# The last residual addition of a fused block, moved from GpSimd into an adding DMA

## The chip, the cores and the metric

The kernel runs on one core of one Trainium2 chip. The metric is the device time of one launch in microseconds (us), lower is better. A profile of one execution on the chip stands beside the times; lines such as L2083 are lines of the kernel before.

## What is computed

The input x has 8192 tokens of 512 numbers in float32. Two halves follow one another, each with a norm before it, a norm behind it and the residual:

```python
x = x + layernorm(attn(layernorm(x)))   # after this line x is called x1 here
x = x + layernorm(ffn(layernorm(x)))    # this is the output
```

`attn` is a gated state mixer: an input projection to u and v, silu of v, a depthwise convolution over three tokens, a linear recurrence along the tokens, a gate u * silu(y), an output projection with a bias, the residual of its own input and a layer norm with weight and bias. `ffn` is 512 to 2048 to 512 with weights made ternary (-1, 0, 1) on the chip, biases and an exact gelu between. The last line is where the change lies: output = x1 + norm of the FFN's result.

## The kernel before, in words

The tokens are cut into NT = 16 tiles of 512, each tile into NB = 4 blocks of 128 tokens (the partitions). A program of stages s runs over the tiles; in stage s four tiles are in work at once, given by `tiles(s)`: tile fa = s-2 is in the FFN, tile c = s-1 in the attention half, tile n = s+1 is loaded, normed and projected, and tile e = s-3 is finished. Each engine has its own list of instructions in a fixed order; times such as AT_F_NORM only set the order in which the list is written. Engines wait for each other by semaphores alone, with constants.

TensorE does all matmuls: `f1` (512 to 2048, reads the transposed operand x3T), `f2` (2048 to 512, into four PSUM banks f2b), and for the attention half `u`, `v` and `o`. Activations are split into a high and a low float16 part, so each product is done twice (three times in the attention half). VectorE makes the low parts (`lo`, L807), statistics, the taps and scan of the recurrence, the norms, and x1 (L963). ScalarE does gelu, high parts, silu, and the affine forms of norms. GpSimd does small scales (L2037, L2038), the carried states (L2088), the output projection's bias (`add_bias`, L2093) and the last addition (`finish`, L2083). SyncE issues all DMAs.

Two buffers matter. `xs` has X_SLOTS = 4 slots, one per tile in flight: x is loaded there, VectorE writes x1 over it (semaphore x1_ok), then makes the norm of x1 in `hb` (n3_ok), which is split, transposed by DMA into x3T and read by f1 of the next stage. `hb` has four blocks and is used in turns: first by tile c (residual copy by ScalarE, L1661, bias, output of `o`, norms), later by tile e: VectorE writes the FFN's result from PSUM (`f_add`, L820), ScalarE norms it in place (`ffn_norm`, L1631, semaphore fn_ok), GpSimd adds x1 from xs in place (`finish`, semaphore fin_ok), SyncE stores it (`store`, L398, semaphore out_st), and only after that store may ScalarE write the residual copy of the next tile c into the block (L1660 waits for out_st).

SyncE's order in a stage is: four stores of tile e, each waiting for its addition; the load of tile n = e+4 into the slot of tile e (`load_x`, L362, waits for all four additions); four transposes of the first operand of tile n; four transposes of x3 of tile c (L414). The last tile is different: its last addition is done by VectorE (`last_sum`, `last_out`, semaphore fin_last) and its stores come at the end.

Of the kernel before, what the change touches and what calls it, by code (L numbers as in the profile page):

```python
# [27 lines left out]
NB = TT // P  # L28
# [63 lines left out]
def build(nc, x, w_in, w_out, w1t, w2t, params, rows, out):  # L92
# [23 lines left out]
    with ExitStack() as ctx:  # L116
# [3 lines left out]
        def sem(name):  # L120
# [99 lines left out]
        w1_in = [sem(f"w1_in{q}") for q in range(4)]  # L220
        w2_in = [sem(f"w2_in{i}") for i in range(4)]
        w1_back, w2_back = sem("w1_back"), sem("w2_back")
        out_st = [sem(f"out_st{i}") for i in range(NB)]

        const_ok, prep, pmx, pm1, scale_ok = sem("const_ok"), sem("prep"), sem("pmx"), sem("pm1"), sem("scale_ok")
# [24 lines left out]
            sem("x1_ok"), sem("n3_ok"), sem("x3_hi"), sem("x3_lo"))  # L250

        f2_sum, fin_last, xc_ok, cen_ok = sem("f2_sum"), sem("fin_last"), sem("xc_ok"), sem("cen_ok")
        f1_mm, gelu_ok, hh_ok, hl_ok, f2_mm, f_ok, fn_ok, fin_ok = (
            sem("f1_mm"), sem("gelu_ok"), sem("hh_ok"), sem("hl_ok"), sem("f2_mm"), sem("f_ok"),
            sem("fn_ok"), sem("fin_ok"))

        def tiles(s):

# [99 lines left out]
        @block.sync  # L358
        def _(sp):
            def load_x(t):  # L360
                if t >= X_SLOTS:
                    sp.wait_ge(fin_ok, NB * (t - X_SLOTS + 1))  # L362
                if t == X_SLOTS - 1:
                    sp.wait_ge(w_ok, last_of(W1_CHUNK, range(8, 12)))
                sp.dma_start(xs[:, t % X_SLOTS, :, :], x_d[t]).then_inc(x_in[t % X_SLOTS], 16)

            def load_w1(q):

                sp.dma_start(w1_raw[q], w1_d[q]).then_inc(w1_in[q], 16)

            def load_w2(group):

                if group == 0:
                    sp.wait_ge(abs_ok, 4)
                elif group == 1:
                    sp.wait_ge(x1_lo, 3 * NB)
                elif group == 2:
                    sp.wait_ge(win_l, 2 * KC)
                else:
                    sp.wait_ge(wo_l, KC)  # L380
                sp.dma_start(w2_raw[group], w2_d[group]).then_inc(w2_in[group], 16)

            def reload_w1():

                sp.wait_ge(w_ok, last_of(W2_CHUNK, range(4, 8)))
                sp.dma_start(w1_kept[3], w1_d[3]).then_inc(w1_back, 16)

            def reload_w2():

                sp.wait_ge(w_ok, last_of(W2_CHUNK, range(8, 12)))  # L390
                sp.dma_start(w2_kept[3], w2_d[3]).then_inc(w2_back, 16)

            def store(t, j):
                if t < NT - 1:
                    sp.wait_ge(fin_ok, NB * t + j + 1)
                else:
                    sp.wait_ge(fin_last, j + 1)
                sp.dma_start(out_d[t, j], hb[:, j, :]).then_inc(out_st[j], 16)  # L398

            def transpose(kind, t, j):  # L400

                if kind == "t1":
                    dst, split = x1T[:, t % 2], x1_lo
                    if t > 1 and j == 0:
                        sp.wait_ge(u_mm, KC * (t - 1))
                else:
                    dst, split = x3T_of(t), x3_lo
                    if t == NT - 2 and j == 0:
                        sp.wait_ge(u_mm, KC * (t + 1))
                    elif t > 0 and j == 0:  # L410
                        sp.wait_ge(f1_mm, FC * min(t, NT - 2))
                r = block_no[kind, t, j] % T_SLOTS
                sp.wait_ge(split, NB * t + j + 1)
                sp.dma_start_transpose(dst[:, :, j * P:(j + 1) * P],  # L414
                                       tp[:, r].rearrange("p h d -> p (h d)")).then_inc(transposed[r], 16)

            def transposes(kind, t):
                for j in range(NB):
                    transpose(kind, t, j)

            sp.dma_start(par[:, :], params).then_inc(par_in, 16)
            for j in range(NB):
                sp.dma_start(xs[:, 0, j, :], x_d[0, :, j, :]).then_inc(x0_in[j], 16)
            for k in range(KC):
                sp.dma_start(wf[:, k, D:], w_in_d[:, k, D:]).then_inc(win_in[k], 16)
            for i in range(2):
                sp.dma_start(xs[:, 1, 2 * i:2 * i + 2, :], x_d[1, :, 2 * i:2 * i + 2, :]).then_inc(x1_in[i], 16)
            transposes("t1", 0)
            for i in range(2):
                sp.dma_start(wf[:, 2 * i:2 * i + 2, 0:D], w_in_d[:, 2 * i:2 * i + 2, 0:D]).then_inc(winu_in[i], 16)  # L430
            transposes("t1", 1)
            load_x(2)
            sp.dma_start(wo_raw, w_out_d).then_inc(wout_in, 16)
            load_w1(0)
            load_w1(1)
            sp.dma_start(row[:, :, :], rows.partition_broadcast(P)).then_inc(row_in, 16)
            load_w1(2)
            load_w1(3)
            load_w2(2)
            transposes("t1", 2)  # L440
            load_w2(0)
            load_w2(1)
            load_w2(3)
            load_x(3)
            reload_w1()
            transpose("t1", 3, 0)
            transpose("t1", 3, 1)
            transpose("t1", 3, 2)
            transpose("t1", 3, 3)
            reload_w2()  # L450
            transpose("t3", 1, 0)
            transpose("t3", 1, 1)
            transpose("t3", 1, 2)
            transpose("t3", 1, 3)
            for s in range(3, NT + 2):
                _, c, n, e = tiles(s)
                if e is not None:
                    for j in range(NB):
                        store(e, j)
                    if e + X_SLOTS < NT:  # L460
                        load_x(e + X_SLOTS)
                if n is not None:
                    transposes("t1", n)
                if c is not None:
                    transposes("t3", c)
            for j in range(NB):
                store(NT - 1, j)
            for j in range(NB):
                sp.wait_ge(out_st[j], 16 * NT)


        @block.tensor
# [1129 lines left out]
        def _(act):  # L1602
# [50 lines left out]
            def residual(c, j):  # L1653

                if c == NT - 1:
                    act.wait_ge(fin_ok, NB * (NT - X_SLOTS + 1))
                else:
                    act.wait_ge(x3_lo, NB * (c - 1) + j + 1)
                if 1 < c < NT - 1:
                    act.wait_ge(out_st[j], 16 * (c - 1))  # L1660
                act.activation(hb_of(c)[:, j, :], xs[:, c % X_SLOTS, j, :], ACT.Identity, bias=nm1[:, c % 4, j:j + 1],  # L1661
                               scale=rs1[:, c % 4, j:j + 1]).then_inc(res_ok, 1)
# [362 lines left out]
        def _(pool):  # L2025
# [54 lines left out]

            def finish(e, j):
                pool.wait_ge(fn_ok, NB * e + j + 1)
                pool.tensor_tensor(hb[:, j, :], hb[:, j, :], xs[:, e % X_SLOTS, j, :], ALU.add).then_inc(fin_ok, 1)  # L2083

            def keep_state(c, b):
                i = KC * c + b
# [183 lines left out]
```

## Time and profile before

| | us |
|---|---|
| median of 3 runs | 1421.73 |
| lowest and highest run | 1421.04, 1422.21 |
| span of the profiled execution, first to last instruction | 1420.3 |
| own time of the profiled execution beside its span | not given by the page |
| TensorE busy | 1400.8 |
| VectorE busy | 1116.8 |
| ScalarE busy | 878.2 |
| GpSimd busy | 422.3 |
| mean granted TensorE clock | 0.999 |
| DMA traffic | 82.00 MB |

The times are those of the whole launch; the profile is of one execution. Busy time is the union of an engine's instruction intervals. Matmuls overlap in the pipeline: one is shown with 0.38 us, while the next starts 0.22 us later. DMA issues are listed as the queue of the engine that issues them (SPq for SyncE), with the time from issue to landing.

### The profile page before, as it was taken

To read this page: it belongs to the slowest core of one execution; us is meant where nothing else is said; L and a number is where in the kernel's file an instruction comes from. 1 tells how busy PE (TensorE), PEld (TensorE's weight loads), DVE (VectorE), ACT (ScalarE), POOL (GpSimd) and SP (SyncE) were. 2 spreads that over 40 slices of the span, in tenths; PEclk is the share of its full clock that TensorE was granted. 3 is DMA by queue.
4 is the path that set the end of the run, shared out by engine and by line. 5 is a ranking of instruction groups with operands and counts; after the bars stand their busy time and mean duration, and the time that the engine had idled before them with its cause. 6 is when DMAs were issued, how large, how long until landed. Compare 5 with 4: busy or idle time off the path is not lost.

```text
span 1420.3 us, 18989 instructions
## 1 busy us (share of the span) xinstructions
PE 1400.8 (99%) x6506; PEld 640.0 (45%) x6506; DVE 1116.8 (79%) x1889; ACT 878.2 (62%) x1264; POOL 422.3 (30%) x522
## 2 busy tenths in 40 slices
PE   7999999999999999999999999999999999999997
PEld 4444444444444444444444444444444444444443
DVE  7999987868779686796867878677796877998744
ACT  7999665656556565675656756565565656753443
POOL 5234241322314232042331413223142321523221
PEclk9999999999999999999999999999999999999999
DMA  8703221211311122121311203113111221001200
GB/s 245 254 36 90 60 83 20 78 30 38 82 30 60 30 61 59 30 66 25 89 30 31 82 16 82 31 38 82 31 60 30 53 67 30 30 1 30 60 31 30
DMA packets 155984, 82.00 MB, mean 58 GB/s; under 512 B 132720, under 2 KB 132720, under 8 KB 155760
## 3 DMA queue, kind: packets, MB, share of 16 engines
q1 hardware_dynamic: 155888, 80.79, 22.0%
q8 instruction: 51, 0.84, 0.2%
q14 instruction: 45, 0.37, 0.1%
HBM read 31.49 MB, written 16.78 MB: 34 GB/s over the span
## 4 chain that ended last, share of the span: by engine, by line
PE 85%; DVE 4%; issue 3%; POOL 1%; ACT 0%; POOLq 0%; DVEq 0%; ACTq 0%
PE f2b L581 14%; PE f2b L582 14%; PE f1b L552 14%; PE f1b L553 14%; PE misc L520 6%; PE misc L519 6%; PE misc L518 6%; PE misc L533 3%; PE misc L534 3%; PE misc L532 3%; DVE bn L789 1%; DVE vl L865 0%; DVE vl L874 0%; DVE ring L807 0%; POOL rsc L2038 0%
## 5 line engine op out<-in xcount | busy, mean ns | idle before, releaser
L581 PE MATMUL f2b<-w,ring 128*128 128x512 fp8e5 x1004 | 380.5, 379 | 1.2 <-DVE ring L807 0.9
L582 PE MATMUL f2b<-w,ring 128*128 128x512 fp8e5 x1004 | 380.5, 379 | 0.0
L552 PE MATMUL f1b<-x3T,w 128*128 128x512 f16 x960 | 363.8, 379 | 0.1
L553 PE MATMUL f1b<-x3T,w 128*128 128x512 f16 x960 | 363.8, 379 | 0.0
L1610 ACT ACTIVATE ring<-f1b,par 128x512 f32<-128x512 f32 x256 | 175.2, 684 | 227.8 <-PE f1b L553 227.5
L2037 POOL TENSOR_SCALAR ve<-mv 128x4 f32<-128x4 f32 (+2 forms) x89 | 35.4, 398 | 725.5 <-DVE mv L799 725.4
L807 DVE SCALAR_TENSOR_TENSOR ring<-ring,f_sc 128x512 f16<-128x512 f32 x256 | 212.5, 844 | 37.6 <-ACT ring L1620 37.4
L1620 ACT ACTIVATE ring<-ring,f_sc 128x512 f16<-128x512 f32 x256 | 180.1, 710 | 0.0
L518 PE MATMUL misc<-x1T,win_hi 128*128 128x512 f16 x456 | 172.8, 379 | 0.0
L520 PE MATMUL misc<-x1T,win_lo 128*128 128x512 f16 x456 | 172.8, 379 | 0.0
L519 PE MATMUL misc<-x1T,win_hi 128*128 128x512 f16 x456 | 172.8, 379 | 0.0
L581 PEld LDWEIGHTS f2b<-w,ring 128*128 128x128 f16 x1004 | 98.2, 98 | 121.1 <-DVE ring L807 2.4
L582 PEld LDWEIGHTS f2b<-w,ring 128*128 128x128 f16 x1004 | 98.2, 98 | 118.0
L552 PEld LDWEIGHTS f1b<-x3T,w 128*128 128x128 fp8e5 x960 | 93.9, 98 | 114.4 <-issue 1.5
L553 PEld LDWEIGHTS f1b<-x3T,w 128*128 128x128 fp8e5 x960 | 93.9, 98 | 112.7
L1729 ACT ACTIVATE vb<-misc,par,inv_sig 128x512 f32<-128x512 f32 x54 | 41.9, 776 | 140.3 <-PE misc L520 140.1
L789 DVE BATCH_NORM_STATS2 bn<-hb 128x6 f32<-128x512 f32 x184 | 118.8, 679 | 0.2
L865 DVE SCALAR_TENSOR_TENSOR vl<-vb,par,vl 128x512 f32<-128x512 f32 x128 | 105.9, 866 | 0.9 <-POOL vb L2142 0.8
L2093 POOL TENSOR_TENSOR hb<-hb,row 128x512 f32<-128x512 f32 x56 | 80.7, 1444 | 85.7 <-ACT hb L1661 85.7
L2083 POOL TENSOR_TENSOR hb<-hb,xs 128x512 f32<-128x512 f32 x60 | 99.6, 1687 | 18.6 <-ACT hb L1631 18.6
L532 PE MATMUL misc<-wo_hi,g_hi 128*128 128x512 f16 x240 | 91.0, 379 | 0.4 <-DVE g_lo L909 0.3
L533 PE MATMUL misc<-wo_lo,g_hi 128*128 128x512 f16 x240 | 91.0, 379 | 0.0
(227 smaller groups left out, 2015.3 us busy)
## 6 DMA issues: line engine op xcount, KB each, us to landing
out_dram<-hb SPq DMA_DIRECT2D x64, 256.0 KB, 2.0
xs<-x_dram SPq DMA_DIRECT2D x14, 1024.0 KB, 5.4
ring<-w1t_dram SPq DMA_DIRECT2D x3, 1024.0 KB, 13.2
stage<-w2t_dram SPq DMA_DIRECT2D x3, 1024.0 KB, 8.0
x1T<-tp SPq DMA_TRANSPOSE x68, 3.1
xs<-x_dram SPq DMA_DIRECT2D x4, 256.0 KB, 3.4
stage<-w_in_dram SPq DMA_DIRECT2D x4, 256.0 KB, 5.7
xs<-x_dram SPq DMA_DIRECT2D x2, 512.0 KB, 7.2
```

The lines of the kernel that those rows point to most:

```text
L518: pe.matmul(o[:, :], wh, x1T[:, s_, k, :], start=k == 0, stop=False)
L519: pe.matmul(o[:, :], wh, x1T[:, s_, KC + k, :], start=False, stop=False)
L520: mm = pe.matmul(o[:, :], wl, x1T[:, s_, k, :], start=False, stop=k == KC - 1)
L532: pe.matmul(out_[:, :], g_hi[:, k, js], wo_hi[:, k, :], start=c > 0 and k == 0, stop=False)
L533: pe.matmul(out_[:, :], g_hi[:, k, js], wo_lo[:, k, :], start=False, stop=False)
L552: pe.matmul(b[:, :], w, src[:, k, :], start=k == 0, stop=False)
L553: mm = pe.matmul(b[:, :], w, src[:, KC + k, :], start=False, stop=k == KC - 1)
L581: pe.matmul(f2b[q][:, :], h_hi[:, i % H_SLOTS, qs], w2[:, j, :], start=j == 0, stop=False)
L582: mm = pe.matmul(f2b[q][:, :], h_lo[:, i % H_SLOTS, qs], w2[:, j, :], start=False, stop=j == FC - 1)
L807: ve_.scalar_tensor_tensor(out=h_lo[:, i % H_SLOTS, :], in0=gg[:, i % G_SLOTS, :], scalar=f_sc[:, 0:1], in1=h_hi[:, i % H_SLOTS, :], op0=A ...
L1610: act.activation(gg[:, i % G_SLOTS, :], f1b[i % 2][:, :], ACT.Gelu, bias=par[:, B1 + j:B1 + j + 1], scale=1.0 / ACT_SCALE).then_inc(gelu_o ...
L1620: act.activation(h_hi[:, i % H_SLOTS, :], gg[:, i % G_SLOTS, :], ACT.Copy, scale=f_sc[:, 0:1]).then_inc(hh_ok, 1)
```

## The change

Before, tile e's result was normed in `hb`, x1 was added to it there by GpSimd, and the sum was stored. Now SyncE stores x1 itself to the output as soon as VectorE has made it (`store_x1`), in the stage in which tile c = s-1 is in the attention half. Two stages later GpSimd issues, for each block, a DMA that adds the normed FFN result from `hb` onto what stands in the output (`accum_op=ALU.add`); before issuing it waits for fn_ok as before and for the landing of that block's x1 store. The landing of the adding DMA now counts out_st. The last tile keeps its old way, with a semaphore of its own (last_st). Since GpSimd no longer reads `xs`, the load of tile t into a slot waits only for the norm (n3_ok) and the x1 store (x1_st) of the tile before in that slot; the same holds for the residual copy of the last tile, which uses a slot of xs.

```diff
--- before.py
+++ after.py
@@ -220,6 +220,8 @@
         w1_in = [sem(f"w1_in{q}") for q in range(4)]
         w2_in = [sem(f"w2_in{i}") for i in range(4)]
         w1_back, w2_back = sem("w1_back"), sem("w2_back")
+        x1_st = [sem(f"x1_st{i}") for i in range(NB)]
+        last_st = [sem(f"last_st{i}") for i in range(NB)]
         out_st = [sem(f"out_st{i}") for i in range(NB)]
 
         const_ok, prep, pmx, pm1, scale_ok = sem("const_ok"), sem("prep"), sem("pmx"), sem("pm1"), sem("scale_ok")
@@ -250,9 +252,9 @@
             sem("x1_ok"), sem("n3_ok"), sem("x3_hi"), sem("x3_lo"))
 
         f2_sum, fin_last, xc_ok, cen_ok = sem("f2_sum"), sem("fin_last"), sem("xc_ok"), sem("cen_ok")
-        f1_mm, gelu_ok, hh_ok, hl_ok, f2_mm, f_ok, fn_ok, fin_ok = (
+        f1_mm, gelu_ok, hh_ok, hl_ok, f2_mm, f_ok, fn_ok = (
             sem("f1_mm"), sem("gelu_ok"), sem("hh_ok"), sem("hl_ok"), sem("f2_mm"), sem("f_ok"),
-            sem("fn_ok"), sem("fin_ok"))
+            sem("fn_ok"))
 
         def tiles(s):
 
@@ -359,7 +361,9 @@
         def _(sp):
             def load_x(t):
                 if t >= X_SLOTS:
-                    sp.wait_ge(fin_ok, NB * (t - X_SLOTS + 1))
+                    sp.wait_ge(n3_ok, NB * (t - X_SLOTS + 1))
+                    for j in range(NB):
+                        sp.wait_ge(x1_st[j], 16 * (t - X_SLOTS + 1))
                 if t == X_SLOTS - 1:
                     sp.wait_ge(w_ok, last_of(W1_CHUNK, range(8, 12)))
                 sp.dma_start(xs[:, t % X_SLOTS, :, :], x_d[t]).then_inc(x_in[t % X_SLOTS], 16)
@@ -390,12 +394,16 @@
                 sp.wait_ge(w_ok, last_of(W2_CHUNK, range(8, 12)))
                 sp.dma_start(w2_kept[3], w2_d[3]).then_inc(w2_back, 16)
 
-            def store(t, j):
-                if t < NT - 1:
-                    sp.wait_ge(fin_ok, NB * t + j + 1)
-                else:
-                    sp.wait_ge(fin_last, j + 1)
-                sp.dma_start(out_d[t, j], hb[:, j, :]).then_inc(out_st[j], 16)
+            def store_x1(t):
+
+                for j in range(NB):
+                    sp.wait_ge(x1_ok, NB * t + j + 1)
+                    sp.dma_start(out_d[t, j], xs[:, t % X_SLOTS, j, :]).then_inc(x1_st[j], 16)
+
+            def store_last(j):
+
+                sp.wait_ge(fin_last, j + 1)
+                sp.dma_start(out_d[NT - 1, j], hb[:, j, :]).then_inc(last_st[j], 16)
 
             def transpose(kind, t, j):
 
@@ -442,31 +450,34 @@
             load_w2(1)
             load_w2(3)
             load_x(3)
+            store_x1(0)
             reload_w1()
             transpose("t1", 3, 0)
             transpose("t1", 3, 1)
             transpose("t1", 3, 2)
             transpose("t1", 3, 3)
             reload_w2()
+            store_x1(1)
             transpose("t3", 1, 0)
             transpose("t3", 1, 1)
             transpose("t3", 1, 2)
             transpose("t3", 1, 3)
             for s in range(3, NT + 2):
                 _, c, n, e = tiles(s)
-                if e is not None:
-                    for j in range(NB):
-                        store(e, j)
-                    if e + X_SLOTS < NT:
-                        load_x(e + X_SLOTS)
+                if e is not None and e + X_SLOTS < NT:
+                    load_x(e + X_SLOTS)
                 if n is not None:
                     transposes("t1", n)
+                if c is not None and c < NT - 1:
+                    store_x1(c)
                 if c is not None:
                     transposes("t3", c)
             for j in range(NB):
-                store(NT - 1, j)
+                store_last(j)
             for j in range(NB):
-                sp.wait_ge(out_st[j], 16 * NT)
+                sp.wait_ge(x1_st[j], 16 * (NT - 1))
+                sp.wait_ge(out_st[j], 16 * (NT - 1))
+                sp.wait_ge(last_st[j], 16)
 
 
         @block.tensor
@@ -1653,7 +1664,8 @@
             def residual(c, j):
 
                 if c == NT - 1:
-                    act.wait_ge(fin_ok, NB * (NT - X_SLOTS + 1))
+                    act.wait_ge(n3_ok, NB * (NT - X_SLOTS + 1))
+                    act.wait_ge(x1_st[j], 16 * (NT - X_SLOTS + 1))
                 else:
                     act.wait_ge(x3_lo, NB * (c - 1) + j + 1)
                 if 1 < c < NT - 1:
@@ -2080,7 +2092,8 @@
 
             def finish(e, j):
                 pool.wait_ge(fn_ok, NB * e + j + 1)
-                pool.tensor_tensor(hb[:, j, :], hb[:, j, :], xs[:, e % X_SLOTS, j, :], ALU.add).then_inc(fin_ok, 1)
+                pool.wait_ge(x1_st[j], 16 * (e + 1))
+                pool.dma_start(out_d[e, j], hb[:, j, :], accum_op=ALU.add).then_inc(out_st[j], 16)
 
             def keep_state(c, b):
                 i = KC * c + b
```

## Rows read from the trace of the kernel before

**Rows 1.** The page's busy line: us, share of the span, instructions
```profile
PE 1400.8 (99%) x6506; PEld 640.0 (45%) x6506; DVE 1116.8 (79%) x1889; ACT 878.2 (62%) x1264; POOL 422.3 (30%) x522
```

**Rows 2.** Busy us by stretch, as the first line says
```profile
...
core 0: us, PE busy (x) PEld busy (x) DVE busy (x) ACT busy (x) POOL busy (x), PEclk, DMA share, GB/s
425.70:512.00 86.30, 86.30 (x401) 39.14 (x400) 67.09 (x112) 52.60 (x76) 24.72 (x30) 1.00 0.20 49
170.00:1400.00 1230.00, 1228.55 (x5688) 555.71 (x5687) 949.10 (x1569) 731.92 (x1064) 354.34 (x414) 1.00 0.19 46
1400.00:1420.30 20.30, 12.87 (x60) 5.66 (x58) 11.69 (x20) 4.74 (x7) 5.56 (x14) 0.92 0.14 52
```

**Rows 3.** Groups by line: busy us, mean ns, idle us before
```profile
...
L2083 POOL TENSOR_TENSOR hb<-hb,xs 128x512 f32<-128x512 f32 x60 | 99.6, 1687 | 18.6 <-ACT hb L1631 18.6
...
L2093 POOL TENSOR_TENSOR hb<-hb,row 128x512 f32<-128x512 f32 x56 | 80.7, 1444 | 85.7 <-ACT hb L1661 85.7
```

**Rows 4.** GpSimd in order of time: start, us, [idle before <- releaser]
```profile
...
437.60 6.76 POOL L2083 TENSOR_TENSOR hb<-hb,xs 128x512 f32<-128x512 f32 x4 [0.93 <-ACT hb L1631]
...
458.91 0.56 POOL L2037 TENSOR_SCALAR ve<-mv 128x4 f32<-128x4 f32 x1 [8.29 <-DVE mv L799]
```

**Rows 5.** SyncE's queue in order of time, 425.7 to 512
```profile
...
438.90 5.82 SPq L398 DMA_DIRECT2D out_dram<-hb  x4
444.76 0.43 SPq L365 DMA_DIRECT2D xs<-x_dram  x1
...
504.20 5.53 SPq L414 DMA_TRANSPOSE x3T<-tp  x4
```

**Rows 6.** VectorE's line L807: ns min/median/max
```profile
...
L807 DVE SCALAR_TENSOR_TENSOR ring<-ring,f_sc x256: 710/739/1756, 97.5 to 1404.5; 128x512 f16<-128x512 f32 x128
```

**Rows 7.** Transpose at 1026.5, its landing, TensorE behind it
```profile
...
L414 SPq DMA_TRANSPOSE x3T<-tp x1: 1822/1822/1822, 1026.5 to 1026.5; - x1
...
DMA to landing us min/median/max: 3.7/3.7/3.7
...
1029.98 0.38 PE L582 MATMUL f2b<-w,ring 128*128 128x512 fp8e5 x1
1030.45 0.38 PE L552 MATMUL f1b<-x3T,w 128*128 128x512 f16 x1
```

**Rows 8.** DMA issues: KB each, median us to landing
```profile
...
out_dram<-hb SPq DMA_DIRECT2D x64, 256.0 KB, 2.0
xs<-x_dram SPq DMA_DIRECT2D x14, 1024.0 KB, 5.4
```

**Rows 9.** ScalarE in order of time, one stage
```profile
...
436.71 1.52 ACT L1631 ACTIVATE hb<-hb,nm,rs 128x512 f32<-128x512 f32 x2 [0.17 <-POOL nm L2069]
...
463.40 0.80 ACT L1661 ACTIVATE hb<-xs,nm,rs 128x512 f32<-128x512 f32 x1
...
470.10 0.80 ACT L1661 ACTIVATE hb<-xs,nm,rs 128x512 f32<-128x512 f32 x1
```

**Rows 10.** VectorE in order of time, the same stage
```profile
...
477.72 0.75 DVE L928 SCALAR_TENSOR_TENSOR hb<-misc,o_inv,hb 128x512 f32<-128x512 f32 x1 [1.16 <-PE misc L534]
...
495.20 0.74 DVE L963 SCALAR_TENSOR_TENSOR xs<-hb,rsc,xs 128x512 f32<-128x512 f32 x1
```

**Rows 11.** Transpose at 508.4, its landing, TensorE's next f1
```profile
...
L414 SPq DMA_TRANSPOSE x3T<-tp x1: 1340/1340/1340, 508.4 to 508.4; - x1
...
DMA to landing us min/median/max: 3.2/3.2/3.2
...
512.05 0.38 PE L552 MATMUL f1b<-x3T,w 128*128 128x512 f16 x1
```

**Rows 12.** SyncE's queue at the front, the transpose's landing
```profile
...
25.98 1.24 SPq L414 DMA_TRANSPOSE x1T<-tp  x1
27.27 0.58 SPq L365 DMA_DIRECT2D xs<-x_dram  x1
...
DMA to landing us min/median/max: 3.1/3.1/3.1
```

## The prediction, made before the change was run

> **What bounds the kernel now.** I read the profile from the whole down to single instructions. The busy line of the page comes first: TensorE is busy 1400.8 us (99%) of a span of 1420.3, the next engine (VectorE) 79% [rows 1]. The busy times by stretch come second, because an average hides where the idle 19.5 us lie: one whole stage, 425.7 to 512.0, is 86.30 us of TensorE in 86.30; the long middle from 170 to 1400 leaves it idle for 1230.00 - 1228.55 = 1.45 us; the end from 1400 leaves 20.30 - 12.87 = 7.43; the remaining 10.6 lie before 170, in the loading and weight preparation [rows 2]. So the reader sees a kernel in which every other engine works behind TensorE. GpSimd's 60 additions are 99.6 us in total [rows 3].
>
> **What goes.** In each of 15 tiles GpSimd loses 4 additions, 6.76 us together (437.60 to 444.36) [rows 4]. Who waited for them: SyncE's queue, which stored the four blocks and then loaded the next x [rows 5], and, through the stores' landing, ScalarE's residual copy into the same buffer. While they ran, some of VectorE's `lo` instructions were slow: the median is 0.739 us, the longest 1.756 [rows 6]. VectorE gets some microseconds a stage back. That is worth nothing inside a stage whose TensorE is full, and at most the 1.45 us of idle time in the middle all together. I take 0.1 us of gain.
>
> **What comes, on GpSimd.** 60 DMA issues, one for each addition. The trace has no DMA issued by GpSimd, so its time on that engine is bounded from rows of other engines: 0.43 us, SyncE's issue of the x load (its four stores fill 5.82 us only because they wait for the additions in between), and 1.82 us, the longest issue of a transpose [rows 5, 7]. I take 1.3 us, nearer the upper end, since GpSimd's own addition of the same block is 6.76 / 4 = 1.69. Four are 5.2 us in place of 6.76. GpSimd's next task that others wait for starts at 458.91 (the scale of the next x), so even 4 us each would be hidden [rows 4]: 437.60 + 16 = 453.6, and 5.3 us are left for the four one-column state copies that come between. Cost on the path 0. The added wait in front of each, that the x1 store has landed, is for a store of two stages (some 150 us) earlier, so it holds nobody up.
>
> **What comes, in the transfer.** The adding DMA must land before the residual copy of the same block number overwrites `hb`. Plain stores land 2.0 us after issue and 1 MB loads 5.4 [rows 8]; an adding DMA moves 256 KB but must also read its destination, so I take twice a store, 4 us, and keep 2.0 and 5.4 as bounds. The first block is normed from 437.5 on, and the residual copies of the first and the fourth start at 463.40 and 470.10 [rows 9]. With four at 1.3 + 4 us, even one after another, the last lands at 437.6 + 21.2 = 458.8. Cover for the last: 11 us; for the first more than 20. Cost 0.
>
> The Trainium skill (DMA: Bandwidth & Descriptors, Anatomy of one DMA) prices one GpSimd DMA at 2.0 us plus bytes over 436 GB/s; by that estimate a block takes 2.6 us, and the sum stays the same. The skill also has a rule against the change (SBUF: State Buffer, in the box on VectorE blocking DMA): while VectorE runs an instruction in a two-port mode, GpSimd can't write its descriptors, and its DMA waits to the end of that instruction. The two-port candidates here are the plain tensor_scalar instructions, which run near the end of the stage; in the window of the finish VectorE runs scalar_tensor_tensor [rows 6]. If each issue waited for one instruction of 1.756 us, four would be 7 us late, inside the 11 of cover. So rule and row differ only in the size of a hidden cost.
>
> **What moves on SyncE.** (a) Four x1 stores a tile are issued once x1 exists: the last is written by VectorE at 495.20 + 0.74 = 495.9, the first transpose of the next operand is issued at 504.20 [rows 5, 10]. With 0.43 us for an issue and 2.0 to land, they are done by 498.4. Cover 5.8 us; without it, each microsecond would be one microsecond of TensorE. (b) The four stores at 438.90 vanish from SyncE's queue, and with them the wait for the additions, behind which the x load stood. (c) The x load of the next tile loses its wait altogether: it is issued right behind the fourth transpose of x3, some 20 us earlier in the stage. That gains nothing: its old landing (444.76 + 5.4 = 450.2) was already ahead of GpSimd's scale for that tile at 458.91 [rows 4, 5]. The queue's count is the same plus the 60 adding DMAs, which go to a queue of GpSimd; 15.7 MB more are written and as many read back, against a DMA share of 0.19 in the middle [rows 2], so that even twice the traffic would leave more than half of the DMA engines' time idle.
>
> **The narrow place** is (c). The fourth transpose is issued at 508.4 and lands 3.2 us later, at 511.6; TensorE's first f1 matmul of the next tile starts at 512.05, without a gap [rows 11]. How much room is that? One stage answers: there the landing took 3.7 us from 1026.5, and the f1 matmul came 0.47 us after its predecessor instead of 0.22, a gap of 0.25 [rows 7]. So the room is 3.7 - 3.2 - 0.25 = 0.25 us. A 1 MB load placed directly behind the transpose could use it up. The nearest row speaks against it: at 25.98 a transpose was followed at 27.27 by a 1 MB x load, the very order of the change, and landed in 3.1 us [rows 12]. From below the cost is 0, since nothing lands earlier by it; from above, a landing as late as the load's own 5.4 would cost 12 x (5.4 - 3.2 - 0.25) = 23 us, for the loads of tiles 4 to 15. I take 0, going by the row with the same order.
>
> **The sum.** -0.1 (VectorE) + 0 (GpSimd issue) + 0 (landing) + 0 (stores and loads on SyncE) on a span of 1420.3 gives 1420.2. The profile gives no other time for its execution; the median of the runs shown is 1421.73, so 1.4 us are put down to what lies around the span. Together 1421.6, which is 0.1 under that median.
>
> **Rivals.**
> 1. *The x load delays the last x3 transpose (slower).* Place: the stage border, 12 times. It decides from 0.25 us of delay. At 0.5 us it costs 12 x 0.25 = 3.0, at 1.0 us 9.0: 1424.7 to 1430.7. For it: almost no room. Against it: [rows 12]. Chance 0.10.
> 2. *The adding DMA is slow and the residual copy waits (slower).* The fourth residual copy at 470.10 may slip until its own 0.80 us and its bias addition on GpSimd (1.44) still meet VectorE's use at 477.72 [rows 3, 9, 10]: to 475.5. So it decides from (475.5 - 437.6) / 4 = 9.5 us a block. At 12 us a block the fourth lands at 485.6, 10 us late in each of 13 stages: about 1550. For it: no such DMA in the trace. Against it: it would have to be nearly twice the landing of a transfer four times as large. Chance 0.07.
> 3. *A first DMA queue of GpSimd costs something once, at start or end.* Nothing in the trace prices it; by the nearest rows, one more landing of 3.2 to 5.4 us that nobody overlaps: 1424.8 to 1427.0. Chance 0.08.
> 4. *Faster.* All idle time of the middle gives 1.45 us, which isn't told from no change; over 2.8 us would have to come from the front or from the tail, whose last tile is unchanged. Chance 0.03, at about 1418.
> The forecast itself has 0.72.
>
> **From these to the numbers.** What a measurement of this kernel can tell from no change is about 0.2%, 2.8 us, so 1418.9 to 1424.6. Forecast: same, 0.72. Slower: rivals 1 to 3, 0.25. Faster: 0.03. The range runs from 1420.0 (all the idle time of the middle gone) to 1427.5, which takes in rival 3 and the smaller half of rival 1 and leaves out some 15 in 100.
>
> **What would show it.** In the changed profile: TensorE's busy time within 1 us of 1400.8, and its idle time in 170 to 1400 below 2 us. GpSimd's line for the additions is gone; VectorE's busy sum is lower by 20 to 50 us, its `lo` mean (844 ns before) nearer 740. The adding DMAs land within 5.4 us, and ScalarE's residual copies show no wait for a DMA. SyncE issues the x load next to the last x3 transpose, whose landing stays at 3.2 to 3.3. I am wrong if a wait of TensorE for those transposes appears in more than one stage (rival 1), if ScalarE waits at the residual copy (rival 2), or if the time around the span grows beyond 1.4 us or the first or last instruction shifts (rival 3).

## The result, and the profile after

| us | median | lowest to highest | runs |
|---|---|---|---|
| before | 1421.73 | 1420.95 to 1423.32 | 5 |
| changed | 1427.57 | 1423.8 to 1428.16 | 5 |

The ratio is 1.0035 (interval 1.0023 to 1.0047): the change makes the kernel slower, by 3.3 to 6.7 us. The forecast was no change, at 1421.6 and between 1420.0 and 1427.5; the median lies 6.0 us above the first and 0.07 us outside the range. The profiled run took 1426.89 us with a span of 1425.1, so 1.8 us lie around the span; its span is 4.8 us longer than that of before. The busy line of the page, of the changed kernel:

```profile
PE 1400.9 (98%) x6506; PEld 639.3 (45%) x6506; DVE 1064.8 (75%) x1889; ACT 876.7 (62%) x1264; POOL 369.7 (26%) x522
```

TensorE's busy time is what it was, 1400.8 then [rows 1] and 1400.9 now, so all that was lost is idle time of TensorE. Where it lies shows in busy times by stretch, of the changed kernel (length, then busy time and instructions of PE, PEld, DVE, ACT and POOL, granted clock, DMA share, GB/s):

```profile
0.00:12.00 12.00, 2.90 (x12) 2.63 (x12) 6.29 (x15) 6.93 (x12) 4.50 (x19) 1.00 0.77 258
12.00:30.00 18.00, 16.89 (x85) 10.91 (x86) 16.18 (x43) 15.16 (x23) 11.21 (x22) 1.00 0.89 189
30.00:60.00 30.00, 30.00 (x137) 14.10 (x136) 27.37 (x54) 26.20 (x39) 7.36 (x17) 1.00 0.80 288
60.00:100.00 40.00, 39.24 (x207) 18.83 (x206) 38.90 (x78) 38.43 (x52) 10.11 (x16) 1.00 0.32 96
100.00:170.00 70.00, 67.73 (x312) 30.13 (x311) 66.71 (x111) 54.00 (x72) 26.78 (x21) 1.00 0.40 108
170.00:1400.00 1230.00, 1228.37 (x5687) 555.72 (x5686) 895.46 (x1569) 730.38 (x1063) 304.10 (x414) 1.00 0.27 57
1400.00:1425.10 25.10, 15.76 (x74) 6.93 (x71) 13.89 (x25) 5.64 (x8) 5.61 (x14) 0.88 0.11 42
```

and of the kernel before, the one stretch that the prediction did not look at by itself:

```profile
100.00:170.00 70.00, 69.81 (x325) 31.41 (x323) 66.88 (x115) 54.43 (x72) 29.26 (x21) 1.00 0.29 76
```

The reader sees that the steady stages lose nothing: 1230.00 - 1228.37 = 1.63 us of idle time against 1.45 [rows 2]. Two places lose. From 100 to 170 TensorE is idle 2.27 us against 0.19, and from 1400 to the end 25.10 - 15.76 = 9.34 against 7.43 [rows 2]. That is 2.08 + 1.91 = 4.0 of the 4.8 us; 0.6 more lie before 30 us (10.21 us of idle time against 9.65), where no instruction differs and where single runs differ by more: in the profiles of all kernels here, those 30 us hold from 9.10 to 11.95 us of idle time of TensorE.

**The end.** The rows at which GpSimd and SyncE close the block, of the changed kernel (duration in ns, start in us) and, behind it, the same of the kernel before. A drain is the instruction with which an engine's program ends here; what it waits for inside isn't shown by the trace.

```profile
L116 POOLq DRAIN  x1: 6069/6069/6069, 1418.8 to 1418.8; - x1
L116 SPq DRAIN  x1: 13/13/13, 1423.0 to 1423.0; - x1
L116 SPq EVENT_SEMAPHORE  x1: 17/17/17, 1425.0 to 1425.0; - x1
```

```profile
L116 POOLq DRAIN  x1: 1129/1129/1129, 1415.9 to 1415.9; - x1
L116 SPq DRAIN  x1: 7/7/7, 1420.1 to 1420.1; - x1
L116 SPq EVENT_SEMAPHORE  x1: 17/17/17, 1420.3 to 1420.3; - x1
```

Before, GpSimd's drain takes 1.13 us and is over at 1417.0, three microseconds ahead of SyncE, which has waited for the last store. Changed, it takes 6.07 us, from 1418.8 to 1424.9. SyncE is through at 1423.0 and the program ends at 1425.0 instead of some 0.2 us behind SyncE. Before, a drain could have taken 1420.1 - 1415.9 = 4.2 us without being seen; 6.07 is 1.9 over that. Price: 1.9 us, once.

**Stage 2.** TensorE's waits, of the changed kernel (what it waited for, us in total, times, longest):

```profile
PE f1b L599 <- ACT tp L1716: 8.2, 1, 8.2
PE misc L543 <- DVE hb L939: 1.9, 1, 1.9
PE f2b L604 <- DVE wm_sq L1035: 1.0, 1, 1.0
...
PE f1b L563 <- DMA x3T<-tp: 0.5, 1, 0.5
```

The second is new. It is one wait: the output projection waits for VectorE to empty a PSUM bank of the `misc` set (`hb` at L939).

```profile
125.91 0.39 PE L543 MATMUL misc<-wo_hi,g_hi 128*128 128x512 f16 x1 [1.92 <-DVE hb L939]
```

Why VectorE is late is read from three engines side by side. SyncE, before and changed (start, duration in us):

```profile
106.30 0.37 SPq L365 DMA_DIRECT2D xs<-x_dram  x1
120.50 0.37 SPq L386 DMA_DIRECT2D stage<-w1t_dram  x1
```

```profile
106.59 0.37 SPq L369 DMA_DIRECT2D xs<-x_dram  x1
107.01 2.64 SPq L401 DMA_DIRECT2D out_dram<-xs  x4
123.25 0.39 SPq L390 DMA_DIRECT2D stage<-w1t_dram  x1
```

Behind the load of x for tile 3 now stand the four x1 stores of tile 0 (`store_x1(0)`). The load lands 6.6 us after its issue instead of 5.1; the rows of its landing, before and changed:

```profile
DMA to landing us min/median/max: 5.1/5.1/5.1
```

```profile
DMA to landing us min/median/max: 6.6/6.6/6.6
```

VectorE and GpSimd, before and changed (in brackets the idle time just before and who ended it):

```profile
112.52 0.68 DVE L789 BATCH_NORM_STATS2 bn<-xs 128x6 f32<-128x512 f32 x1
115.76 2.73 DVE L909 SCALAR_TENSOR_TENSOR g_lo<-yb,g_sc,g_hi 128x512 f16<-128x512 f32 x4
118.41 2.06 DVE L1192 SCALAR_TENSOR_TENSOR w<-stage,thr,w 128x512 fp8e5<-128x512 f32 x3
117.72 5.13 POOL L2093 TENSOR_TENSOR hb<-hb,row 128x512 f32<-128x512 f32 x2 [5.08 <-ACT hb L1661]
```

```profile
113.22 0.69 DVE L800 BATCH_NORM_STATS2 bn<-xs 128x6 f32<-128x512 f32 x1 [0.33 <-DMA xs<-x_dram]
116.47 3.75 DVE L920 SCALAR_TENSOR_TENSOR g_lo<-yb,g_sc,g_hi 128x512 f16<-128x512 f32 x4
120.14 3.08 DVE L1203 SCALAR_TENSOR_TENSOR w<-stage,thr,w 128x512 fp8e5<-128x512 f32 x3
118.09 1.57 POOL L2106 TENSOR_TENSOR hb<-hb,row 128x512 f32<-128x512 f32 x1 [5.16 <-ACT hb L1673]
120.91 1.76 POOL L2106 TENSOR_TENSOR hb<-hb,row 128x512 f32<-128x512 f32 x1 [1.24 <-ACT hb L1673]
```

VectorE's statistics wait 0.33 us for the load, and VectorE is 0.7 us later than before (0.3 of it was there already, since the load itself is issued 0.29 us later). By an estimate from these rows that alone would cost TensorE nothing: 2.7 us of lateness, below, cost it 1.9, so some 0.8 are free. But it turns round who gets its data first, as GpSimd is only 0.37 us later and its first bias addition so starts 1.62 us into the `g_lo` group in place of 1.96. Before, GpSimd's two bias additions are stretched to 5.13 us and VectorE runs its two groups in 2.73 and 2.06. Changed, GpSimd's additions run in 1.57 and 1.76, and each of VectorE's groups takes 1.02 us longer. So VectorE comes out 2.7 us late (123.14 against 120.40 for the next statistics), and TensorE stands. This is the pattern that the Trainium skill states (SBUF: State Buffer, "Who interferes with whom"): a VectorE instruction with two SBUF inputs and a GpSimd instruction that reads SBUF share a pair of ports, and "Issue order, not op shape, decides who blocks." The rows agree in that only one of the two is slow at a time, with 1.0 us a group as the price for VectorE and about 1.8 for GpSimd, whose two took 5.13 instead of 3.33. No run takes the ports themselves apart.

### The profile page after: what moved, and what is told of

It reads as the page before. It is cut to its first block, busy times and chain, and to the rows that moved or that the text cites. A ratio compares the mean times of both kernels' runs of the same rounds, so it can differ in the third digit from the quotient of the medians.

```text
span 1425.1 us, 19081 instructions
## 1 busy us (share of the span) xinstructions
PE 1400.9 (98%) x6506; PEld 639.3 (45%) x6506; DVE 1064.8 (75%) x1889; ACT 876.7 (62%) x1264; POOL 369.7 (26%) x522
## 4 chain that ended last, share of the span: by engine, by line
PE 83%; DVE 5%; issue 2%; ACT 1%; DMA 1%; POOL 1%; POOLq 0%; SPq 0%; DVEq 0%; ACTq 0%
PE f1b L563 14%; PE f1b L564 14%; PE f2b L592 14%; PE f2b L593 14%; PE misc L531 6%; PE misc L530 6%; PE misc L529 6%; PE misc L543 3%; PE misc L545 3%; PE misc L544 3%; DVE bn L800 1%; DVE w L1203 1%; DVE g_lo L920 0%; DMA xs<-x_dram 0%; DVE vl L876 0%
## 5 line engine op out<-in xcount | busy, mean ns | idle before, releaser
L818 DVE SCALAR_TENSOR_TENSOR ring<-ring,f_sc 128x512 f16<-128x512 f32 x256 | 184.8, 736 | 41.8 <-ACT ring L1631 41.8
L885 DVE TENSOR_TENSOR_SCAN vl<-a_par,carry,vl 128x512 f32<-128x512 f32 x60 | 77.3, 1291 | 28.6 <-issue 15.5
L876 DVE SCALAR_TENSOR_TENSOR vl<-vb,par,vl 128x512 f32<-128x512 f32 x128 | 92.7, 761 | 1.0 <-POOL vb L2155 0.8
L543 PE MATMUL misc<-wo_hi,g_hi 128*128 128x512 f16 x240 | 91.0, 379 | 2.3 <-DVE hb L939 1.9
```

The lines of the kernel that those rows point to most:

```text
L543: pe.matmul(out_[:, :], g_hi[:, k, js], wo_hi[:, k, :], start=c > 0 and k == 0, stop=False)
L818: ve_.scalar_tensor_tensor(out=h_lo[:, i % H_SLOTS, :], in0=gg[:, i % G_SLOTS, :], scalar=f_sc[:, 0:1], in1=h_hi[:, i % H_SLOTS, :], op0=A ...
```

## The experiments

Each kernel ran beside the kernel before on the same chip. The medians of before were 1422.07 (33 runs) beside the first four kernels, 1422.32 (34) beside the second four and 1422.22 (27) beside the last four; each experiment has 10 to 12 runs, the last one 5.

### First: is it the drain, is it the stores of tile 0, and can each be made or unmade alone?

**e1_no_drain.** The changed kernel without GpSimd's drain at the end.

```diff
-        block = ctx.enter_context(nc.Block())
+        block = ctx.enter_context(nc.Block(no_gpsimd_drain=True))
```

> The changed kernel, with GpSimd's drain at the end of the program left out (an option of the block that ends it; all adding DMAs are still waited for by semaphore). Theory A (the loss has two places: GpSimd's end-of-program drain, 6.07 us in place of 1.13, which ends 1.9 us after SyncE's, and the x1 store of tile 0 behind the x load of tile 3, where TensorE waits 1.9 us): the tail loses about 1.9 us, the time is 1425.4 to 1425.9 where the changed kernel has 1427.6, the wait at the o projection stays. Rival B (the adding DMAs cost by their traffic or by the new queue as such, everywhere a little): the time stays at 1427 or more, since the end only waits for the transfers themselves.

Measured 1425.04 (ratio 1.0019, interval 1.001 to 1.0027). In its profile there is no drain row of GpSimd, SyncE is through at 1422.5 and the program ends at 1422.7; the wait at L543 stays at 1.9 us. What is left is 1425.04 - 1422.07 = 3.0 us (1.4 to 3.8 by the interval), and it holds the wait in stage 2, for which 2.1 to 2.5 was expected.

**e2_x1_of_tile0_late.** The changed kernel with the stores of tile 0 behind the transposes of tile 3.

```diff
             load_x(3)
-            store_x1(0)
             reload_w1()
...
             transpose("t1", 3, 3)
+            store_x1(0)
             reload_w2()
```

> The changed kernel, with the four x1 stores of tile 0 moved from behind the x load of tile 3 to behind the four transposes of tile 3. Theory A: the x load of tile 3 lands in 5.1 us again (6.6 in the changed kernel), VectorE doesn't wait for it, TensorE's wait of 1.9 us before the o projection of tile 1 is gone; time lower by 2.1 to 2.5 us, about 1425.3. Rival B: no change, since the same bytes are moved. A third possibility (C): the wait comes from a shift of GpSimd's work against VectorE's that some 0.3 us at the start cause already; then the wait stays, with the x load landing in 5.1.

Measured 1424.17 (1.0016, 1.0007 to 1.0025). The load lands in 5.1 us again, and the rows of stage 2 are those of before:

```profile
111.82 0.68 DVE L800 BATCH_NORM_STATS2 bn<-xs 128x6 f32<-128x512 f32 x1
115.06 2.73 DVE L920 SCALAR_TENSOR_TENSOR g_lo<-yb,g_sc,g_hi 128x512 f16<-128x512 f32 x4
117.71 2.06 DVE L1203 SCALAR_TENSOR_TENSOR w<-stage,thr,w 128x512 fp8e5<-128x512 f32 x3
117.01 5.14 POOL L2106 TENSOR_TENSOR hb<-hb,row 128x512 f32<-128x512 f32 x2 [5.07 <-ACT hb L1673]
```

The wait at L543 is gone, TensorE is busy 69.80 of the 70 us from 100 to 170, and the drain still takes 6.07 us. What is left is 2.1 us, against the 1.9 of the drain. Theory C of the expectation, that the wait would stay with the load in time, is out.

**e3_before_x1_store.** The kernel before, with only the stores of tile 0's x1 added at their place; nothing else of the change, and its own stores of that tile later wait for them.

```diff
             load_x(3)
+            for j in range(NB):
+                sp.wait_ge(x1_ok, j + 1)
+                sp.dma_start(out_d[0, j], xs[:, 0, j, :]).then_inc(x1_st[j], 16)
             reload_w1()
...
```

> The kernel before, with one thing added: SyncE stores the four x1 blocks of tile 0 to the output behind the x load of tile 3 (overwritten later by the real stores). No DMA by GpSimd. Theory A: 2.1 to 2.5 us slower than before, about 1424.0, with TensorE's wait of about 1.9 us before the o projection of tile 1. Rival B (it takes the adding DMAs or their queue): within 0.3 us of before.

Measured 1424.4 (1.0012, 1.0003 to 1.002). Its load is issued at 105.96, 0.3 us earlier than before, and lands 6.7 us later; the rows are those of the changed kernel:

```profile
112.69 0.69 DVE L795 BATCH_NORM_STATS2 bn<-xs 128x6 f32<-128x512 f32 x1 [0.44 <-DMA xs<-x_dram]
115.94 3.75 DVE L915 SCALAR_TENSOR_TENSOR g_lo<-yb,g_sc,g_hi 128x512 f16<-128x512 f32 x4
117.56 1.58 POOL L2099 TENSOR_TENSOR hb<-hb,row 128x512 f32<-128x512 f32 x1 [5.26 <-ACT hb L1667]
```

with a wait of TensorE of 2.0 us at the same matmul. Four stores, and no adding DMA at all, bring 2.3 us of loss by the medians (0.4 to 2.8 by the interval).

**e4_before_one_dma.** The kernel before with one small DMA issued by GpSimd at its start, of 1 KB, into a scratch tensor that nobody reads.

```diff
+            pool.dma_start(probe[:, :], params[:, 0:2]).then_inc(probe_in, 16)
             pool.memset(ident[:, :], 0.0).then_inc(const_ok, 1)
...
```

> The kernel before, with one thing added: one small DMA of 1 KB issued by GpSimd at the very start (128 rows of 8 bytes of the parameters into a scratch tile nobody reads). Theory A in the form that the drain has a fixed price once GpSimd has issued any DMA: GpSimd's drain 6 us, time about 1423.6 (+1.9). In the form that it grows with the DMAs issued: drain near 1.1 us and time within 0.3 of before. Rival B: the same, within 0.3.

Measured 1421.98 (1.0, 0.9991 to 1.0009). GpSimd's drain takes 0.81 us. So it isn't the first use of a DMA queue by GpSimd that costs something: one DMA costs nothing that these runs can tell (the interval is 1.3 us to either side). Only the time around the span is a little longer, 1.9 to 2.0 us in all its runs where the kernel before has 1.8.

### Second: do the two add up, and is it the drain itself or the order of VectorE?

**f1_changed_again.** The changed kernel, unchanged, beside the others.

> The changed kernel once more, unchanged, so that the runs beside it are compared with it on one chip. Theory A and its rivals alike: 1427 us, 5 us over before, GpSimd's drain 6.07 us at the end, TensorE's wait of 1.9 us at the o projection of tile 1.

Measured 1426.11 (1.0023, 1.0014 to 1.0032), 3.8 us over before (2.0 to 4.6 by the interval), where 5 was expected. The drain takes 6.08 us, the wait at L543 is 1.7.

**f2_both_undone.** The edits of e1_no_drain and e2_x1_of_tile0_late together.

> The changed kernel with both places mended: the x1 stores of tile 0 behind the transposes of tile 3, and no GpSimd drain at the end. Theory A: the two are independent and add up, 1.9 + 2.5 us less than the changed kernel, 1422.3 to 1422.8, within 0.1% of before. A rival that something else spread over the stages costs (traffic, descriptor work beside VectorE): 1 us or more over before stays, with idle time of TensorE between 170 and 1400 above 1.9.

Measured 1422.22 (1.0003, 0.9994 to 1.0011): level with before, within 0.9 us below to 1.6 above. The two causes are all of it that these runs can tell, and they add up.

**f3_drain_early.** The late stores of e2_x1_of_tile0_late, and an explicit drain on GpSimd behind the adding DMAs of tile 14, when nobody waits for GpSimd; the drain at the end stays.

```diff
                     items += [(0, lambda j=j: finish(e, j)) for j in range(NB)]
+                    if e == NT - 2:
+                        items += [(1, lambda: pool.drain())]
```

> The changed kernel with the x1 stores of tile 0 late, and one more drain instruction on GpSimd behind the last adding DMAs (tile 14, near 1375 us), the one at the end kept. Theory D (the drain clears what the 60 DMAs left behind, once): the early one takes some 5 to 6 us unseen, the last one 1.1 us or less; time as in the kernel with both places mended, about 1422.5. Theory E (the drain is long whenever GpSimd has issued such DMAs, however long ago): the last one still takes 6 us, time as with the late stores alone, 1424.2.

Measured 1422.7 (0.9999, 0.9991 to 1.0008). Its two drains:

```profile
L2233 POOLq DRAIN  x1: 8597/8597/8597, 1373.1 to 1373.1; - x1
L116 POOLq DRAIN  x1: 1146/1146/1146, 1417.2 to 1417.2; - x1
```

The early one takes 8.6 us, beside other work; it begins together with the last issue (1373.1), so part of it may be the landing of the last DMAs (up to 7.2 us in this run). The last one is back at 1.15. What the drain does for the adding DMAs it does once; whoever asks early pays nothing at the end that these runs can tell.

**f4_stats_later.** The changed kernel; VectorE takes the statistics of tile 3's first block, which need the load, four instructions later.

```diff
             ternary(16)
-            x_stats(3, 0)
             lo(0, 4)
...
             gate(1, 3)
+            x_stats(3, 0)
             gate_lo(1, 0)
```

> The changed kernel with one VectorE instruction moved: the first statistics of x tile 3 come after the three gate instructions instead of before `lo`, so VectorE doesn't stand at the x load that lands 1.5 us late. The stores stay where they are. If the late load matters only through that stand (0.4 us) and what the shift does to VectorE's order against GpSimd's bias addition: the g_lo group is 2.7 us for four again (3.75 in the changed kernel), TensorE's wait at the o projection is gone, time 2.1 to 2.5 us less, about 1425. If the stores' traffic itself costs (slower operands, later reload of w1): no change.

Measured 1423.7 (1.0006, 0.9997 to 1.0014), 2.4 us under the changed kernel beside it and 1.4 over before, with the drain at 6.08 us. The load still lands 6.7 us after its issue, since the stores still stand behind it, but nobody waits for it:

```profile
114.89 0.68 DVE L800 BATCH_NORM_STATS2 bn<-xs 128x6 f32<-128x512 f32 x1
115.50 2.71 DVE L920 SCALAR_TENSOR_TENSOR g_lo<-yb,g_sc,g_hi 128x512 f16<-128x512 f32 x4
117.43 5.13 POOL L2106 TENSOR_TENSOR hb<-hb,row 128x512 f32<-128x512 f32 x2 [5.06 <-ACT hb L1673]
```

and TensorE's wait at L543 for `hb` is gone. So the chain runs by this one wait: the slow landing without the wait costs nothing.

### Third: what is left, and what the drain counts

**g1_stats_later_no_drain.** The changed kernel with the edits of f4_stats_later and e1_no_drain.

> The changed kernel with the statistics of x tile 3 moved behind the gate instructions and without GpSimd's drain at the end: both costs mended, the first in the other way. Theory A: 1.9 us below the kernel with the moved statistics alone (1423.7), so 1421.6 to 1422.0, which is level with before or up to 0.5 below it. If the two places are not independent: above 1422.8.

Measured 1421.96 (0.9995, 0.9986 to 1.0004). Both causes undone in another way give the kernel before again. It can't be told from the one before.

**g2_before_no_drain.** The kernel before with the option of e1_no_drain.

> The kernel before without GpSimd's drain at its end. Its drain (1.13 us from 1415.9) ends 3 us before SyncE's own end, so theory A expects no change, within 0.3 us. If the option itself makes the end of a program cheaper, the two kernels without the drain would have flattered theory A: then this one is 1 us or more faster than before.

Measured 1423.89 (1.0005, 0.9996 to 1.0014; 1420.99 to 1426.65). The interval holds no change, but the median is 1.7 us over before, which wasn't expected. Of that, 0.2 lie around the span, which is 2.0 to 2.1 us in all its runs. The profile is of its slowest run, 1426.65. In that run the load of x took 6.4 us to land, with no store behind it:

```profile
113.34 0.69 DVE L789 BATCH_NORM_STATS2 bn<-xs 128x6 f32<-128x512 f32 x1 [0.17 <-DMA xs<-x_dram]
116.59 3.75 DVE L909 SCALAR_TENSOR_TENSOR g_lo<-yb,g_sc,g_hi 128x512 f16<-128x512 f32 x4
118.30 1.49 POOL L2093 TENSOR_TENSOR hb<-hb,row 128x512 f32<-128x512 f32 x1 [5.08 <-ACT hb L1661]
```

and TensorE waited 1.8 us. Of the 4.3 us by which this span is longer than that of before, 2.2 lie in this stretch (100 to 170), 0.9 before 30 us and 0.9 in 170 to 1400, where TensorE waits 1.1 us for a transpose of x3. Since the code up to here is that of the kernel before, that kernel stood on the edge already: a load that lands late by itself pushes it over. How often that happens, and whether it makes this median, one profile doesn't show. The option by itself saves nothing there, as the drain was over three microseconds before the end.

**g3_before_stats_later.** The kernel before with the statistics later, as in f4_stats_later.

> The kernel before with the first statistics of x tile 3 moved behind the gate instructions on VectorE. Here the x load lands in time, so theory A expects no change (within 0.3 us), and the g_lo group stays at 2.7 us. If the move is a gain by itself, this is 0.5 us or more faster than before, and the kernel with the moved statistics says less about the late load.

Measured 1421.98 (0.9998, 0.9989 to 1.0007), all runs between 1421.16 and 1423.0. In its profile the load landed in 6.3 us as well, the `g_lo` group took 2.71 and TensorE didn't wait. So the edit took away the edge in this run. It gains nothing in the median, but none of its 11 runs is over 1423.0, where 7 of the 27 of before are.

**g4_sixty_small_dmas.** The kernel before with 60 DMAs of 1 KB by GpSimd, one behind each addition, each waiting for the landing of the one before.

```diff
+                pool.wait_ge(probe_in, 16 * (NB * e + j))
+                pool.dma_start(probe[:, :], params[:, 0:2]).then_inc(probe_in, 16)
...
```

> The kernel before with a small DMA (128 rows of 8 bytes into a scratch tile) issued by GpSimd behind each of its 60 additions. If GpSimd's drain at the end grows with the number of DMAs it has issued: 6 us as with the 60 adding DMAs (0.81 with one), time about 1424. If it grows with bytes or comes from adding: about 1.1 us, time within 0.5 of before.

Measured 1431.95 (1.0066, 1.0053 to 1.0078), where about 1424 was expected. The end:

```profile
L116 POOLq DRAIN  x1: 5641/5641/5641, 1424.3 to 1424.3; - x1
L116 SPq DRAIN  x1: 7/7/7, 1428.2 to 1428.2; - x1
L116 SPq EVENT_SEMAPHORE  x1: 17/17/17, 1430.1 to 1430.1; - x1
```

The drain takes 5.64 us after 60 small DMAs, nearly as much as the 6.07 after 60 of 256 KB; in both kernels the last of them had landed over 35 us before the drain began. So the drain grows with what GpSimd has issued, and the 256-fold bytes account for at most the 0.43 us between the two; nor is it what is still in flight. Both kinds have 128 rows a DMA, so whether it counts DMAs or rows stays open, and 1 and 60 are the only numbers tried. It costs 1.7 us here (5.64 over the 1428.2 - 1424.3 = 3.9 that stay unseen). The other 8.0 us (1431.95 - 1422.22 - 1.7) were not meant, and the larger part shows in TensorE's waits, of the same kernel (before, this wait is 0.9 us in two):

```profile
PE f2b L583 <- DVE ring L809: 6.3, 13, 0.8
```

The waits for the small DMAs spread the four additions from 439.2 to 447.4 us in the stage where they ran from 437.6 to 444.4 before [rows 4], so that they met VectorE's `lo` instructions at other moments; the mean of `lo` rose from 844 to 877 ns, and TensorE waited for it about half a microsecond, 13 times. That this is again GpSimd's instructions in VectorE's way, through the same ports, is argued from the likeness, not shown.

## Why the prediction was wrong, by its own steps

**Right: the steady stages.** TensorE's busy time within 0.1 us of before, idle time from 170 to 1400 at 1.63 (below 2 was said). VectorE's busy sum fell by 1116.8 - 1064.8 = 52 us (20 to 50 was said, so a little more) and the mean of `lo` from 844 to 736 ns ("nearer 740"), and that bought nothing, as said. The issues and landings, of the changed kernel (ns, minimum, median and maximum; then landing in us):

```profile
L2096 POOL DMA_DIRECT2D out_dram<-hb x60: 853/1036/1181, 181.5 to 1374.8; - x60
...
DMA to landing us min/median/max: 3.9/5.2/7.1
```

An issue takes 1.04 us where 1.3 was taken. A landing takes 5.2 where 4 was taken, and up to 7.1, beyond the upper bound of 5.4; with 11 us of cover the error costs nothing. The x1 store that an adding DMA waits for is not some 150 us earlier, as the prediction has it: by its own rows it is 437.6 + 2 x 86.3 - 495.9 = 114, and nobody waits either way. The Trainium skill's price (DMA: Bandwidth & Descriptors, Anatomy of one DMA) gives 2.6 us for such a block; the trace has twice that for a DMA that adds, and the measurement decides. The rule of the Trainium skill that VectorE in a two-port mode holds up GpSimd's descriptors (SBUF: State Buffer, the box weighed in the prediction) shows nowhere in these rows: the longest of 60 issues is 1.18 us. That doesn't refute it, because beside the issues looked at (438 to 446 us) VectorE ran scalar_tensor_tensor and the scan, and no plain tensor_scalar.

**Right: the narrow place.** The x load right behind the last x3 transpose did no harm. TensorE waited for x3T once, 0.5 us, at the border where the kernel before had its gap of 0.25 [rows 7], and the median landing of those transposes stayed at 3.3. The profile of f1_changed_again has two such waits, 1.3 and 0.5, which by the prediction's own sign would speak for rival 1; but g2_before_no_drain, with SyncE's old order, has 1.1 and 0.3 at the same two places, so the order isn't their cause. Rival 1 is out, and so is rival 2: ScalarE's residual copies show no wait, for a DMA or anything else (the last number is the idle time before them):

```profile
L1673 ACT ACTIVATE hb<-xs,nm,rs 128x512 f32<-128x512 f32 x56 | 44.5, 799 | 0.0
```

**Wrong: "What moves on SyncE", (a), cost 0.** The cover of the x1 stores was worked out in one steady stage, where no load stands in front of them, and it held in all steady stages. The same function is also called by hand in the opening, for tiles 0 and 1, and the call for tile 0 stands directly behind the 1 MB load of tile 3. That call was in the diff and got no line of the sum. The stores themselves are not late; they make the load late, by 1.5 us, and the load had 1.1 us of room (landed at 106.30 + 5.1 = 111.4, read from 112.52). What is over is 0.4 us; it grew to two microseconds only because it turned round VectorE and GpSimd, a mechanism for which the prediction has no step. Measured: 2.1 us in the profile, and 2.4 as the difference of medians between f1_changed_again and f4_stats_later, in place of 0. e3_before_x1_store makes this part alone and e2_x1_of_tile0_late and f4_stats_later unmake it in two ways. Over all profiles: with the four stores behind it the load took 6.4 to 6.7 us in six of six; without them 5.0 to 5.2 in six of eight, and 6.3 and 6.4 in the other two, for which no cause was found.

**Mis-sized: rival 3.** "Something once, at start or end" is what happens, at the end: 1.9 us, in place of the 3.2 to 5.4 that were taken from the landings, and it is not the first queue that costs it but GpSimd's drain after many DMAs. The sum has no term for the end of the program at all. The chance of the rival was 0.08, because no row of the trace before prices it. The row that was there, GpSimd's drain of 1.13 us from 1415.9, wasn't read; with SyncE through at 1420.1 it shows at what length the drain sets the end, 4.2 us. That the range nearly takes in the result is luck: its upper end was built from this rival's landings and from rival 1, and neither is what happened.

**Mis-sized: the 1.4 us around the span.** In the profiled runs where both are known it is 1.8, but for e4_before_one_dma and g2_before_no_drain (2.0); all runs of before beside the experiments have 1.8 to 1.9. The profiled execution of before was thus about 0.4 us above the median of its runs, and the base of the sum was right only because the term was worked out from that median.

The sum with the measured terms is 1421.7 + 1.9 + 2.1 (to 2.4) = 1425.7 to 1426.0. The changed kernel's medians were 1427.57 and, in the second set, 1426.11 beside 1422.32 for before. Against the second the terms leave nothing open (4.0 to 4.3 for 3.8); against the first 1.6 to 1.9 us are open, of a ratio whose own interval is 3.4 us wide, and part of which is the opening before 30 us, 0.6 us in the profiled run. Whether that part is anything but the spread of runs was not settled; the medians of both kernels with the two causes undone show none of it.

## What to carry to other kernels

When an edit moves a helper that is called in a loop and also by hand in the opening or the tail, each place needs its own line of the sum: a zero from the steady stage says nothing about the others. A transfer that is hidden itself can still delay the one queued ahead of it, so it is to be weighed against the room of its neighbour, and against what that neighbour's reader meets when it starts later. When GpSimd begins to issue many DMAs, its drain at the end can get longer (1.13 us with none, 6.07 with 60); compare its end with that of the last store, and if it comes last, give the engine an explicit drain earlier, while nobody waits for it.

## What the runs showed of the hardware that was not expected

- GpSimd's drain took 1.13 us after no DMA, 0.81 after one, 5.64 after 60 of 1 KB, 6.07 after 60 adding ones of 256 KB, and, asked for early after 60, 8.6 (with the last of them still in flight) and then 1.15 for the second.
- Four stores of 256 KB issued right behind a load of 1 MB went with a landing of 6.4 to 6.7 us in six profiles; without them it was 5.0 to 5.2 in six and 6.3 and 6.4 in two.
- A shift of 0.2 to 0.3 us between two engines goes with some 2 us of TensorE's time: where GpSimd's first bias addition starts 1.93 to 1.96 us into VectorE's `g_lo` group, the additions wait (two take 5.13); where it starts after 1.62 to 1.73 us, VectorE does (1.0 us in each of two groups). Nine profiles show the first, five the second, none a third case.
